# Casting the keys' first bfloat16 part on GpSimd instead of VectorE in a fused gated MLP, attention and MLP block

## The chip, the cores and the metric

The kernel runs on one core of one Trainium2 chip. The metric is the device time of one launch in microseconds (us), the median of several runs. The engines are called as in the profile: PE is TensorE (PEld its weight loads), DVE is VectorE, ACT is ScalarE, POOL is GpSimd and SP is SyncE, which here only starts DMAs.

## The reference

The input is x of shape (32, 128, 128): 32 sequences of 128 tokens of width 128. Two layers follow each other, all in float32:

```
x = x + quantized_down( val * gelu(gate) )          # val, gate = up(x * scale * rsqrt(mean(x*x) + 1e-6))
g1, b1, g2, b2, a1, a2 = condition (six vectors of 128 per sequence)
h = layernorm(x) * g1 + b1
q, k, v = split(h @ W_qkv.T + b_qkv)                # 16 heads of width 8
o = softmax(q @ k.T / sqrt(8)) @ v
x = x + (o @ W_o.T + b_o) * a1
h = layernorm(x) * g2 + b2
x = x + (gelu_tanh(h @ W_f1.T + b_f1) @ W_f2.T + b_f2) * a2
```

## The kernel before

The work is done per sequence b (0 to 31), and in groups g of four sequences (0 to 7) where 512 columns fit one instruction. Three stages follow each other on every engine, and each engine's order is written out by hand as a program of its own, with semaphores between them. An engine carries out its program strictly in order, so an instruction that waits holds up everything behind it on that engine.

The first stage (`gated_mlp(s)`, s from 0 to 38) is the gated MLP with its quantization, one sequence entering per step. It also makes the attention's features for each sequence (POOL normalizes pairs of them into `xn_tile`, L1071, PE transposes them, L580, ACT stores them, L664), and every fourth step POOL computes the next four `rstd0` (L1006), which ACT's `gate` (L695) of the step after it needs. In steps 13, 15, 17, 21 and 23 PE projects the queries, keys or values of groups 0 and 1.

The second stage (`attention(b)`, b from -3 to 32) is attention. It overlaps the end of the first for b from -3 to 3, and from b = 4 it stands alone. Scores are computed twice. One pass (`max_scores`, three sequences ahead) only serves the row maxima (DVE, `mx`, L893). POOL splits the negated maxima into three bfloat16 parts (`split_max`, L1040 to L1046), PE transposes them (`transpose_max`, L434), ACT copies them (`m_T`, L743) and SP sends them by DMA into the stacked queries (L349). The second pass (`exp_scores`) then gives scores less their maxima, ACT takes the exponential (`probs`, L727), PE weighs the values (`weigh`), DVE turns the result (`o_turn`, L900, `rinv`, L903), POOL divides it (`o_norm`, L1094, in `scale_output`) and DVE turns it back (L907). PSUM banks rotate: a pair of banks is filled again only when DVE's maxima or ACT's exponential of its previous fill are done.

float32 queries and keys are multiplied as sums of bfloat16 parts. A group's queries q_f and keys k_f (128x512, float32, written by ACT, L679 and L683) are each split into three parts in `q_part` and `k_part`:

- part 0 is the value rounded to bfloat16: for q by DVE in `cast_q` (L811), for k by DVE in `cast_k` (L818, an addition of a broadcast zero, so with two inputs in SBUF);
- POOL subtracts it (q_rest, L1016; k_rest, L1026), rounds the rest (L1018; L1030) and subtracts again (L1022; L1032).

SP sends the parts into the stacks `q_st` and `k_st` by DMAs (L297 and L301), six rows each, as the parts come ready (`second_q_first_k` waits for `k_cast` before the three DMAs of key part 0; it is entered once per group). There are three stacks, and a group's stacks are first read by `max_scores` some nine us after its parts are made.

In the attention stage this work is spread over the four sequences of a group: with b % 4 = 0 DVE casts q and POOL does L1016 and L1018; with b % 4 = 1 DVE casts k between its two maxima, and POOL does, in this order, `split_max`, `scale_output`, L1022 and L1026; with b % 4 = 2 POOL does `split_max`, `scale_output`, L1030 and L1032; with b % 4 = 3 only the DMAs are left. I call these four positions stage 0, 1, 2 and 3 of a group. Groups 2 to 7 are cast here, at b = 1, 5, 9, 13, 17 and 21. Groups 0 and 1 are cast in the first stage: DVE casts k in steps 16 and 24 at the end of its step, and POOL does L1026 at the end of the same step, behind `ystep` (L1059) and the pair of `xn_tile`.

The third stage is the output projection, the second layer norm and the MLP by groups; it holds none of the changed instructions.

PE's order in one `attention(b)` is: exp scores (b, first half), weigh (b-1, second half), max scores (b+3, first half), a projection if one is due, exp scores (b, second half), weigh (b, first half), max scores (b+3, second half), transpose of the maxima of b+2.

Of the kernel before, what the change touches and what calls it, by code (L numbers as in the profile page):

```python
# [10 lines left out]
ALU = mybir.AluOpType  # L11
# [3 lines left out]
P = 128  # L15
# [7 lines left out]
GRP = 4  # L23
GT = GRP * P
NG = B // GRP
# [7 lines left out]
STACKS = 3  # L33
# [93 lines left out]
SHARED = {f: n for n, f in enumerate(f for f in SHARED_FILLS if f[0] not in ("proj", "res", "norm"))}  # L127
# [10 lines left out]
def build(nc, x, first, early, late, cond, out):  # L138
    x_d = x.rearrange("b t d -> t b d")
    out_d = out.rearrange("b t d -> t b d")  # L140
    with ExitStack() as ctx:
        def sb(name, shape, dt=F32):
            return ctx.enter_context(nc.sbuf_tensor(name, shape, dt))

        def sem(name):
            return ctx.enter_context(nc.semaphore(name))

        def sems(name, n):
            return [sem(f"{name}{k}") for k in range(n)]
# [15 lines left out]
        def wl(name):  # L165
            a, b = LATE_AT[name]
            return w_late[:, a:b]
# [28 lines left out]
        zero_c, eps_c = sb("zero_c", [P, 1]), sb("eps_c", [P, 1])  # L196
# [18 lines left out]
        q_f, k_f = sb("q_f", [D, GT]), sb("k_f", [D, GT])  # L215
        q_rest, k_rest = sb("q_rest", [D, GT]), sb("k_rest", [D, GT])
        q_part, k_part = sb("q_part", [D, 3, GT], BF16), sb("k_part", [D, 3, GT], BF16)
# [22 lines left out]
        def bank(n):  # L240
            return psum[:, n, :]
# [16 lines left out]
        shared_mm, shared_set = sem("shared_mm"), sem("shared_set")  # L258

        q_cast, k_cast, q_step, k_step = sem("q_cast"), sem("k_cast"), sem("q_step"), sem("k_step")  # L260
        q_stacked, k_stacked = sems("q_stacked", STACKS), sems("k_stacked", STACKS)
# [14 lines left out]
        def tile_cols(t, b, n=1):  # L276
            return t[:, b * D:(b + n) * D]
# [4 lines left out]
        def k_done(g):  # L282
            return 16 * 6 * (g // STACKS + 1) + (CONST_DONE if g % STACKS else 0)
# [480 lines left out]
        def _(dve):  # L764
            v = nc.vector
# [16 lines left out]
            def mean_squares(g):  # L782
                v.tensor_scalar(ms[:, g * GRP:(g + 1) * GRP], ssq[:, g * GRP:(g + 1) * GRP], 1.0 / D, 1e-6,
                                ALU.mult, ALU.add).then_inc(ms_set, 1)
# [21 lines left out]
            def cast_q(g):  # L806
                dve.wait_ge(shared_set, SHARED["q", g] + 1)
                if g:
                    dve.wait_ge(q_stacked[(g - 1) % STACKS], q_done(g - 1))
                    dve.wait_ge(q_step, 3 * g)  # L810
                v.tensor_copy(q_part[:, 0, :], q_f[:, :]).then_inc(q_cast, 1)  # L811

            def cast_k(g):
                dve.wait_ge(shared_set, SHARED["k", g] + 1)
                if g:
                    dve.wait_ge(k_stacked[(g - 1) % STACKS], k_done(g - 1))
                    dve.wait_ge(k_step, 3 * g)
                v.tensor_tensor(k_part[:, 0, :], k_f[:, :], zero_c[:, :].to_broadcast([P, GT]), ALU.add).then_inc(k_cast, 1)  # L818

            def gated_mlp(s):  # L820
                if 0 <= s - 2 < B:
                    c, n = s - 2, s % 2
                    dve.wait_ge(a_hintT_mm, c + 1)
                    if c >= 2:
                        dve.wait_ge(a_y_mm, c - 1)
                    v.tensor_scalar(hintT[:, n, :, :].rearrange("p a b -> p (a b)"), bank(5).bitcast(I16)[:, 0:FF], -SHIFT, None,
                                    ALU.add).then_inc(a_hintT, 1)
                if 0 <= s - 4 < B:
                    c = s - 4
                    dve.wait_ge(a_x1, c + 1)  # L830
                    v.bn_stats(stats[:, c % 2, :], tile_cols(x_tok, c)).then_inc(a_stats, 1)
                if s < B:
                    n, m = s % 2, s % 4
                    dve.wait_ge(a_gate, s + 1)
                    dve.wait_ge(a_val_mm, s + 1)
                    if s >= 2:
                        dve.wait_ge(a_hrnd, s - 1)
                    v.scalar_tensor_tensor(hid[:, n, :], bank(3 + n), rstd0[:, s:s + 1], gate[:, n, :], ALU.mult, ALU.mult).then_inc(a_hid, 1)  # L838
                    dve.wait_ge(a_hid, s + 1)
                    v.tensor_reduce(amax[:, m:m + 1], hid[:, n, :], X_AXIS, ALU.max, apply_absolute_value=True).then_inc(a_amax, 1)  # L840
                if s == 0:
                    quantize_down()
                if 0 <= s - 3 < B:
                    c = s - 3
                    xs = tile_cols(x_tok, c)
                    dve.wait_ge(a_y_mm, c + 1)
                    dve.wait_ge(a_ystep, c + 1)
                    v.scalar_tensor_tensor(xs, bank(6)[:, 0:D], ystep[:, c % 8:c % 8 + 1], xs, ALU.mult, ALU.add).then_inc(a_x1, 1)
                if s < B:
                    m = s % 4  # L850
                    dve.wait_ge(a_amax, s + 1)
                    v.tensor_scalar(qstep[:, m:m + 1], amax[:, m:m + 1], 1e-5, 1.0 / 127.0, ALU.max, ALU.mult).then_inc(a_qstep, 1)  # L852
                if 0 <= s - 4 < B:
                    c = s - 4
                    dve.wait_ge(a_stats, c + 1)
                    if c >= 4 and c % 2 == 0:
                        dve.wait_ge(a_xn, c - 2)
                    v.bn_aggr(mv[:, c % 4, :], stats[:, c % 2, :]).then_inc(a_mv, 1)
                if s < B:
                    m = s % 4  # L860
                    dve.wait_ge(a_qstep, s + 1)
                    if s >= 4:
                        dve.wait_ge(a_hrnd, s - 3)
                    v.reciprocal(qscale[:, m:m + 1], qstep[:, m:m + 1]).then_inc(a_qscale, 1)  # L864
                if s == 1:
                    dve.wait_ge(wternT_mm, 1)
                    v.tensor_copy(w_ternT[:, :, :].rearrange("p a b -> p (a b)"), bank(5).bitcast(BF16)[:, 0:FF]).then_inc(wternT_set, 1)
                if s % GRP == 2 and s // GRP + 1 < NG:
                    g = s // GRP + 1
                    dve.wait_ge(sq_set, GRP * g)  # L870
                    mean_squares(g)
                if s == 3:
                    dve.wait_ge(mods_mm, 1)
                    dve.wait_ge(late_loaded, 16)
                    for n in range(6):
                        v.tensor_scalar(mods[:, n, :], bank(MISC_BANK)[:, n * B:(n + 1) * B], wl("b_c")[:, n:n + 1], None, ALU.add).then_inc(mods_set, 1)
                if s == 5:
                    dve.wait_ge(bias_mm, 1)
                    v.tensor_copy(b_qk[:, :], bank(MISC_BANK)[:, 0:2]).then_inc(bias_set, 1)
                    v.tensor_tensor(b_ov[:, :], bank(MISC_BANK)[:, 2:3], wl("b_o"), ALU.add).then_inc(bias_set, 1)  # L880
                if s - 1 in EARLY_PROJ:
                    name, g = EARLY_PROJ[s - 1]
                    if name == "q":
                        cast_q(g)
                    if name == "k":
                        cast_k(g)

            def maxima(c, r):
                pair = PAIRS[OWNER[FILL_AT["max", c, r]]]
# [53 lines left out]
            def attention(b):  # L943
                if 0 <= b - 1 < B:
                    normalize(b - 1)
                if 0 <= b + LEAD < B:
                    maxima(b + LEAD, 0)
                g = (b + 8) // GRP
                if b >= 0 and b % GRP == 0 and g < NG:
                    cast_q(g)  # L950
                if b >= 0 and b % GRP == 1 and g < NG:
                    cast_k(g)
                if b == 27:
                    gate_projection(0)
                if b == 28:
                    add_residual(0, MISC_BANK)
                if 0 <= b + LEAD < B:
                    maxima(b + LEAD, 1)
                if 0 <= b - 1 < B:
                    turn_back(b - 1)  # L960
                if b == 28:
                    statistics(0)
                if b == 29:
                    gate_projection(1)
                if b == 30:
                    modulate(0, MISC_BANK)
                    add_residual(1, MISC_BANK)
                    statistics(1)
# [32 lines left out]
        def _(pool):  # L1001
            p = nc.gpsimd
# [19 lines left out]
                p.tensor_tensor(q_part[:, 2, :], q_rest[:, :], q_part[:, 1, :], ALU.subtract).then_inc(q_step, 1)  # L1022

            def k_rest_first(g):
                pool.wait_ge(k_cast, g + 1)
                p.tensor_tensor(k_rest[:, :], k_f[:, :], k_part[:, 0, :], ALU.subtract).then_inc(k_step, 1)  # L1026

# [137 lines left out]
```

## Time and profile before

| | |
|---|---|
| median of 3 runs | 319.92 us (319.9 to 320.2) |
| the profiled execution | 319.64 us |
| its span, first to last instruction | 317.8 us |
| PE busy | 279.6 us (88%) |
| DVE busy | 246.6 us (78%) |
| ACT busy | 186.3 us (59%) |
| POOL busy | 178.6 us (56%) |
| mean granted clock of PE | 0.983 of full speed |

The profile is one execution. Starts are us from the span's start. A granted clock of 1.00 is 2.4 GHz, 0.50 is 1.2 GHz. Matmul ends are modelled, and neighbouring instructions of one engine may overlap by some hundredths of a us in the listing. In a row of the timeline, the bracket says how long the engine had been idle before the instruction and whose work ended that idle time.

### The profile page before, as it was taken

To read this page: it belongs to the slowest core of one execution; us is meant where nothing else is said; L and a number is where in the kernel's file an instruction comes from. 1 tells how busy PE (TensorE), PEld (TensorE's weight loads), DVE (VectorE), ACT (ScalarE), POOL (GpSimd) and SP (SyncE) were. 2 spreads that over 40 slices of the span, in tenths; PEclk is the share of its full clock that TensorE was granted. 3 is DMA by queue.
4 is the path that set the end of the run, shared out by engine and by line. 5 is a ranking of instruction groups with operands and counts; after the bars stand their busy time and mean duration, and the time that the engine had idled before them with its cause. 6 is when DMAs were issued, how large, how long until landed. Compare 5 with 4: busy or idle time off the path is not lost.

```text
span 317.8 us, 8220 instructions
## 1 busy us (share of the span) xinstructions
PE 279.6 (88%) x2892; PEld 154.6 (49%) x2892; DVE 246.6 (78%) x650; ACT 186.3 (59%) x347; POOL 178.6 (56%) x357
## 2 busy tenths in 40 slices
PE   3989998898989576999999989888877999999993
PEld 2454454454445344555656565655443455555441
DVE  5679997877899976598989898998955676676432
ACT  4557997687768564676677777675545222333330
POOL 8032684985896669377878696953334444322300
PEclk9999999999999997899999999999979999999999
DMA  7940000430340004335354444520000011011112
GB/s 238 327 102 4 0 1 3 120 87 2 92 116 2 0 10 113 86 78 143 93 142 104 119 108 112 149 72 8 6 3 3 0 33 33 1 35 33 33 35 66
DMA packets 26216, 21.57 MB, mean 68 GB/s; under 512 B 4384, under 2 KB 25536, under 8 KB 25920
## 3 DMA queue, kind: packets, MB, share of 16 engines
q1 hardware_dynamic: 25744, 20.37, 24.0%
q10 hardware_dynamic: 432, 0.67, 0.7%
q8 instruction: 24, 0.39, 0.6%
q14 instruction: 16, 0.13, 0.1%
HBM read 4.26 MB, written 2.10 MB: 20 GB/s over the span
## 4 chain that ended last, share of the span: by engine, by line
PE 46%; POOL 20%; DVE 17%; issue 11%; ACT 4%; DMA 1%; POOLq 0%; DVEq 0%; ACTq 0%
PE psum L274 39%; DVE mx L893 5%; POOL q_rest L1016 3%; POOL q_part L1018 3%; POOL q_part L1022 2%; POOL k_rest L1026 2%; DVE hid L838 2%; POOL o_norm L1094 2%; POOL xn_tile L1071 2%; DVE o_turn L900 1%; ACT sq L703 1%; PE psum L623 1%; DVE projT L912 1%; PE psum L460 1%; POOL m_rest L1042 1%
## 5 line engine op out<-in xcount | busy, mean ns | idle before, releaser
L893 DVE TENSOR_REDUCE mx<-psum 128x8 f32<-128x1024 f32 x64 | 75.9, 1193 | 10.5 <-PE psum L274 10.3
L727 ACT ACTIVATE probs<-psum 128x1024 f32<-128x1024 f32 x64 | 65.4, 1023 | 9.5 <-PE psum L274 7.9
L274 PE MATMUL psum<-w_early,h0T 128*128 128x512 f32 x128 | 69.3, 627 | 0.0
L760 ACT ACTIVATE g_act<-psum,w_late 128x512 f32<-128x512 f32 x32 | 22.0, 688 | 46.4 <-PE psum L274 46.4
L274 PE MATMUL psum<-probs,v_pad 128*32 128x128 f32 x1024 | 42.4, 285 | 3.3 <-DVE o_turn L900 2.8
L274 PE MATMUL psum<-h2T,w_late 128*128 128x512 f32 x64 | 31.3, 605 | 0.0
L274 PEld LDWEIGHTS psum<-probs,v_pad 128*32 128x32 f32 x1024 | 25.2, 111 | 11.0 <-ACT probs L727 4.4
L274 PE MATMUL psum<-g_act,w_late 128*128 128x512 f32 x64 | 28.8, 592 | 0.0
L838 DVE SCALAR_TENSOR_TENSOR hid<-psum,rstd,gate 128x512 f32<-128x512 f32 x32 | 23.7, 739 | 6.2 <-PE psum L274 3.7
L695 ACT ACTIVATE gate<-psum,rstd 128x512 f32<-128x512 f32 x32 | 22.0, 688 | 8.9 <-PE psum L274 8.5
L274 PE MATMUL psum<-q_st,k_st 64*128 64x128 bf16 x512 | 26.2, 224 | 0.6 <-DVE mx L893 0.5
L1071 POOL TENSOR_SCALAR xn_tile<-x_tok,mv,rstd 128x128 f32<-128x128 f32 x32 | 25.7, 809 | 1.7
L274 PE MATMUL psum<-k_st,q_st 64*128 64x128 bf16 x512 | 25.5, 220 | 0.6 <-DVE mx L893 0.6
L710 ACT ACTIVATE hrnd<-hid,qscale 128x512 f32<-128x512 f32 x32 | 22.9, 716 | 4.5 <-DVE qscale L864 4.3
L1059 POOL TENSOR_TENSOR ystep<-qstep,w_step 128x1 f32<-128x1 f32 x32 | 6.1, 192 | 31.5 <-DVE qstep L852 31.5
L840 DVE TENSOR_REDUCE amax<-hid 128x1 f32<-128x512 f32 x32 | 22.0, 686 | 1.1
L274 PEld LDWEIGHTS psum<-q_st,k_st 64*128 64x128 bf16 x512 | 15.2, 96 | 15.1 <-issue 11.4
L274 PEld LDWEIGHTS psum<-w_early,h0T 128*128 128x128 f32 x128 | 20.5, 200 | 3.1 <-issue 3.1
L274 PEld LDWEIGHTS psum<-k_st,q_st 64*128 64x128 bf16 x512 | 14.5, 94 | 13.5 <-issue 11.6
L994 DVE TENSOR_SCALAR yT<-psum,w_late,mods 128x128 f32<-128x128 f32 x32 | 10.9, 403 | 12.7 <-PE psum L274 12.7
L1100 POOL TENSOR_TENSOR var_e<-mv,eps_c 128x4 f32<-128x4 f32 x8 | 1.6, 201 | 33.7 <-DVE mv L932 33.7
L1094 POOL TENSOR_TENSOR o_norm<-o_turn,rinv 128x128 f32<-128x128 f32 x32 | 15.7, 491 | 7.9 <-DVE rinv L903 7.8
(125 smaller groups left out, 541.3 us busy)
## 6 DMA issues: line engine op xcount, KB each, us to landing
q_st<-q_part SPq DMA_DIRECT2D x48, 128.0 KB
k_st<-k_part SPq DMA_DIRECT2D x48, 128.0 KB, 2.4
x_tok<-x SPq DMA_DIRECT2D x8, 256.0 KB, 7.2
out<-out_t SPq DMA_DIRECT2D x8, 256.0 KB, 2.3
w_late<-late SPq DMA_DIRECT2D x1, 1159.5 KB, 9.1
w_early<-early ACTq DMA_DIRECT2D x2, 256.0 KB, 5.4
k_st<-k_st SPq DMA_DIRECT2D x4, 128.0 KB, 4.9
q_st<-q_st SPq DMA_DIRECT2D x4, 128.0 KB
```

What stands on the lines that cost most here:

```text
L274: return nc.tensor.matmul(o, w, m, start=start, stop=stop, skip_group_check=shares)
L695: nc.scalar.activation(gate[:, n, :], bank(1 + n), ACT.Gelu, scale=rstd0[:, s:s + 1]).then_inc(a_gate, 1)
L710: nc.scalar.activation(hrnd[:, n, :], hid[:, n, :], ACT.Copy, bias=ROUND_UP, scale=qscale[:, c % 4:c % 4 + 1]).then_inc(a_hrnd, 1)
L727: nc.scalar.activation(probs[:, n % 3, :, :, :].rearrange("p f j q -> p (f j q)"), psum[:, pair[0]:pair[1] + 1, :].rearrange("p a b -> p ( ...
L760: nc.scalar.activation(g_act[:, f, :], bank(2 + f % 2), ACT.Gelu_apprx_tanh, bias=wl("b_f1")[:, f:f + 1]).then_inc(c_gelu[f], 1)
L838: v.scalar_tensor_tensor(hid[:, n, :], bank(3 + n), rstd0[:, s:s + 1], gate[:, n, :], ALU.mult, ALU.mult).then_inc(a_hid, 1)
L840: v.tensor_reduce(amax[:, m:m + 1], hid[:, n, :], X_AXIS, ALU.max, apply_absolute_value=True).then_inc(a_amax, 1)
L893: v.tensor_reduce(mx[:, c % 2, :, r, :], psum[:, pair[0]:pair[1] + 1, :].rearrange("p f (j k) -> p f j k", j=4), X_AXIS, ALU.max, negate=T ...
L994: last = v.tensor_scalar(yT[:, s, :], bank(5)[:, s * P:(s + 1) * P], wl("b_f2"), mods[:, 5, b:b + 1], ALU.add, ALU.mult)
L1016: p.tensor_tensor(q_rest[:, :], q_f[:, :], q_part[:, 0, :], ALU.subtract).then_inc(q_step, 1)
L1071: p.tensor_scalar(xn_tile[:, n + e, :], tile_cols(x_tok, c + e), mv[:, n + e, 0:1], rstd[:, n + e:n + e + 1], ALU.subtract, ALU.mult).then ...
L1094: p.tensor_tensor(o_norm[:, :, :, :], o_turn[:, :, 0:16].rearrange("p g (e d) -> p g e d", e=2), rinv[:, :, :].unsqueeze(3).to_broadcast([ ...
```

## The change

DVE no longer casts k. POOL makes key part 0 itself, with the same addition of a zero, at the start of `k_rest_first`, so directly in front of L1026. The three waits that DVE had in front of the cast (k_f written, the previous group's key stack complete, the previous group's parts all made) are now POOL's. `k_cast` is still what SP waits for. Nothing else moves.

```diff
-            def cast_k(g):
-                dve.wait_ge(shared_set, SHARED["k", g] + 1)
-                if g:
-                    dve.wait_ge(k_stacked[(g - 1) % STACKS], k_done(g - 1))
-                    dve.wait_ge(k_step, 3 * g)
-                v.tensor_tensor(k_part[:, 0, :], k_f[:, :], zero_c[:, :].to_broadcast([P, GT]), ALU.add).then_inc(k_cast, 1)
-
...
                     if name == "q":
                         cast_q(g)
-                    if name == "k":
-                        cast_k(g)
...
                 if b >= 0 and b % GRP == 0 and g < NG:
                     cast_q(g)
-                if b >= 0 and b % GRP == 1 and g < NG:
-                    cast_k(g)
...
             def k_rest_first(g):
+                pool.wait_ge(shared_set, SHARED["k", g] + 1)
+                if g:
+                    pool.wait_ge(k_stacked[(g - 1) % STACKS], k_done(g - 1))
+                    pool.wait_ge(k_step, 3 * g)
+                p.tensor_tensor(k_part[:, 0, :], k_f[:, :], zero_c[:, :].to_broadcast([P, GT]), ALU.add).then_inc(k_cast, 1)
                 pool.wait_ge(k_cast, g + 1)
                 p.tensor_tensor(k_rest[:, :], k_f[:, :], k_part[:, 0, :], ALU.subtract).then_inc(k_step, 1)
```

## Rows read from the trace of the kernel before

**Rows 1.** The page: busy time of PE, and the chain that ended last, by engine.
```profile
PE 279.6 (88%) x2892; PEld 154.6 (49%) x2892; DVE 246.6 (78%) x650; ACT 186.3 (59%) x347; POOL 178.6 (56%) x357
PE 46%; POOL 20%; DVE 17%; issue 11%; ACT 4%; DMA 1%; POOLq 0%; DVEq 0%; ACTq 0%
```
**Rows 2.** The chain of work that ended last: start us, us, what.
```profile
167.46 1.16 POOL q_rest L1016
...
168.70 1.04 POOL q_part L1018
...
175.16 3.54 PE psum L274 x66
...
182.27 1.16 POOL q_rest L1016
```
**Rows 3.** Waits, whole span: engine, line, releaser, us in total, times, longest.
```profile
PE psum L434 <- POOL m_part L1046: 7.0, 14, 1.9
```
**Rows 4.** Timeline, group 5: start us, us, engine, line, operation, idle before.
```profile
170.13 0.40 PE L274 MATMUL psum<-k_st,q_st 64*128 64x128 bf16 x8
...
170.69 0.68 DVE L818 TENSOR_TENSOR k_part<-k_f,zero_c 128x512 bf16<-128x512 f32 x1
170.69 0.94 POOL L1094 TENSOR_TENSOR o_norm<-o_turn,rinv 128x128 f32<-128x128 f32 x1
...
171.29 1.22 DVE L893 TENSOR_REDUCE mx<-psum 128x8 f32<-128x1024 f32 x1
...
172.71 1.15 POOL L1026 TENSOR_TENSOR k_rest<-k_f,k_part 128x512 f32<-128x512 f32 x1
...
173.30 3.01 SPq L301 DMA_DIRECT2D k_st<-k_part  x3
...
173.82 0.19 POOL L1040 CAST m_part<-mx 128x16 bf16<-128x16 f32 x1
...
174.92 0.24 PE L434 MATMUL psum<-eye_b,m_part 128*64 128x128 bf16 x1 [0.33 <-POOL m_part L1046]
```
**Rows 5.** POOL's second key part and o_norm by line: duration ns min/median/max, first and last start.
```profile
L1030 POOL TENSOR_TENSOR k_part<-k_rest,zero_c x8: 1036/1040/1043, 63.1 to 204.8; 128x512 bf16<-128x512 f32 x8
L1094 POOL TENSOR_TENSOR o_norm<-o_turn,rinv x32: 406/408/945, 122.6 to 243.3; 128x128 f32<-128x128 f32 x32
```
**Rows 6.** Timeline of POOL, ACT and PE around the key cast of group 0.
```profile
60.10 1.73 POOL L1071 TENSOR_SCALAR xn_tile<-x_tok,mv,rstd 128x128 f32<-128x128 f32 x2
...
68.21 1.03 POOL L1006 TENSOR_TENSOR rstd<-ms,half 128x4 f32<-128x4 f32 x1
...
69.64 0.69 ACT L695 ACTIVATE gate<-psum,rstd 128x512 f32<-128x512 f32 x1 [0.25 <-PE psum L274]
...
74.45 1.10 PE L274 MATMUL psum<-feat,wq_h 128*128 128x512 f32 x2 [0.93 <-ACT feat L664]
```
**Rows 7.** Timeline of POOL and PE around the key cast of group 1.
```profile
85.94 1.79 POOL L1071 TENSOR_SCALAR xn_tile<-x_tok,mv,rstd 128x128 f32<-128x128 f32 x2
...
92.42 1.58 POOL L1071 TENSOR_SCALAR xn_tile<-x_tok,mv,rstd 128x128 f32<-128x128 f32 x2
...
93.28 0.33 PE L580 MATMUL psum<-w_first,xn_tile 128*128 128x128 f32 x1 [1.04 <-POOL xn_tile L1071]
```
**Rows 8.** Timeline of PE and POOL around the key cast of group 2.
```profile
122.68 0.32 PE L434 MATMUL psum<-eye_b,m_part 128*64 128x128 bf16 x1 [1.94 <-POOL m_part L1046]
...
129.75 0.24 PE L434 MATMUL psum<-eye_b,m_part 128*64 128x128 bf16 x1
...
131.15 0.20 POOL L1040 CAST m_part<-mx 128x16 bf16<-128x16 f32 x1 [2.19 <-DVE mx L893]
```
**Rows 9.** Windows of the span: busy us (x) by engine, granted PE clock, DMA share, GB/s.
```profile
120.00:122.00 2.00, 0.75 (x24) 0.37 (x15) 2.00 (x3) 0.73 (x1) 1.91 (x4) 1.00 0.72 185
...
124.00:126.00 2.00, 2.00 (x33) 1.19 (x29) 0.46 (x2) 1.41 (x2) 1.78 (x5) 0.50 0.34 88
...
170.00:210.00 40.00, 36.75 (x743) 23.26 (x739) 36.27 (x60) 28.13 (x41) 32.47 (x74) 1.00 0.49 127
```

## The prediction

> **What bounds the kernel now.** I first read the page's busy shares and its chain [rows 1]. PE is busy for 88% of the span, but the chain of work that ended last runs through PE for only 46%, through POOL for 20% and DVE for 17%. POOL is busy for only 56% of the span, yet carries a fifth of the chain: it must be late at certain places. Since this change takes 8 instructions from DVE and gives 8 to POOL, those places decide.
>
> So I read the chain in order of time [rows 2]. In the attention stage it repeats: q_rest starts at 167.46 and again at 182.27, one group of four sequences in 14.81 us, and the same steps stand there for five groups (q_rest at 137.84, 152.65, 167.46, 182.27 and 197.09). Within a group the chain enters POOL at q_rest, stays on it up to k_rest, goes to 3.54 us of PE work, then over DVE's maxima and cast of q back to POOL. The waits view has the hand-over: PE waits 7.0 us in all, 14 times, for POOL's last part of the maxima [rows 3]. The timeline shows where in the group [rows 4]: k_rest runs from 172.71, split_max follows without idle time at 173.82, and PE's transpose at 174.92 has stood idle 0.33 us for it. Everything that makes k_rest end later makes that transpose, and all of PE behind it, later by the same amount. DVE is not in that stretch: its second maxima of stage 1 start at 171.29, right behind the cast of k, though PE's scores for them were done at 170.53 [rows 4]. The cast does hold DVE up there, by 0.6 us, but split_max of the next stage starts only at 173.82, long after these maxima end at 172.51. DVE's time there is cover, POOL's is not.
>
> **The change, part by part.**
>
> *DVE without the cast.* Eight times 0.68 us [rows 4], 5.4 us of busy time. In the attention groups I cost the gain at 0: the maxima get ready 0.6 us earlier for a POOL that comes 1.3 us later. In the first stage DVE waits for PE soon after each of the two casts. What this would be worth if DVE were the bound is a rival below.
>
> *o_norm gets its speed back.* o_norm takes 0.94 us at 170.69, where the cast of k starts on DVE at the same moment [rows 4]; its median over 32 is 0.408 us and its maximum 0.945 us [rows 5]. That is 0.53 us on POOL, in the stretch without idle time that ends at PE's transpose, and so on the path. The change removes the DVE instruction that does it: -0.53 us per group. It is the one thing that speaks for the change. The Trainium skill (SBUF — State Buffer, Who interferes with whom) says that a DVE instruction with two SBUF inputs contends with a GpSimd one that reads SBUF, and that the second to issue fully blocks until the first finishes. By that rule the slip would be up to the cast's whole 0.68 us, which would make the forecast some 0.8 us lower over five groups; the measured duration shows 0.53, and that decides.
>
> *POOL with the cast.* The same form (128x512 bfloat16 from float32, adding the zero) takes POOL 1.040 us, 1.036 to 1.043 [rows 5]. k_rest now also waits for POOL's own preceding instruction. Such a pair in the chain, q_rest at 167.46 with 1.16 us and its follower at 168.70, leave a gap of 0.08 us [rows 2]; an instruction that waits for nothing recent starts some 0.03 us ahead of its predecessor's end (173.82 against 172.71 + 1.15 [rows 4]). So the cast costs 1.04 + 0.11 = 1.15 us of POOL. The three added waits are for things long done (k_f, the last group's stack and steps), and I cost them at 0, between 0 and 0.05 us each group; the first part of the maxima at 173.82 has two satisfied waits and follows its predecessor without a gap [rows 4].
>
> *Groups 3 to 7.* 1.15 - 0.53 = +0.62; worked forward from 170.69 with 0.41, 1.16, 1.04, the gap and k_rest, and overlaps as in the rows, k_rest ends 0.58 us later. I take 0.58: PE's idle time of 0.33 us at the transpose [rows 4] becomes about 0.9. It closes a ring, so each group pays it: 5 x 0.58 = +2.9 us. Bounds: 0.3 a group if the ring has some slack that I don't see, 0.7 if every wait costs.
>
> *Group 2.* PE waits 1.94 us at 122.68 for POOL and then runs at half clock; its next transpose at 129.75 does not wait, and POOL itself is idle 2.19 us before 131.15 [rows 8]. POOL's extra 1.15 us fits into that idle time. A little is won since the DVE cast no longer runs beside POOL: -0.1 us.
>
> *Group 1 (step 24).* The pair of xn_tile at 85.94 takes 1.79 us beside the DVE cast, 1.58 without [rows 7]: -0.21. The cast adds 1.04 + 0.08, together +0.91 us, behind it. From there POOL has no idle time up to the next xn_tile, for which PE already stands idle 1.04 us at 93.28 [rows 7]. All of it is on the path: +0.9 us.
>
> *Group 0 (step 16).* The same sum, 1.12 - 0.15 = +0.97 us on POOL (the pair at 60.10 takes 1.73). POOL's next product that someone waits for is rstd0: it ends at 69.24, and ACT's gate starts at 69.64, released by PE [rows 6]. With 0.97 us more it ends at 70.21, and the gate starts some 0.6 us later. ACT runs without idle time from there until the features that PE's projection at 74.45 has waited 0.93 us for [rows 6]. So +0.6 us; 0 to 0.97 as bounds.
>
> *SP's queue.* key part 0 is ready some 1.8 us later than now, at about 173.2. SP gets to its wait for k_cast after the two DMAs of q, and starts the keys' DMAs at 173.30 [rows 4]. The queue's own work hides it: 0. If that cover fails, the maxima's DMA behind it moves by a few tenths, and its reader comes two sequences later.
>
> **Sum:** 2.9 - 0.1 + 0.9 + 0.6 = +4.3 us. The sum is made against the profiled execution, 319.64 us, which is 0.3 us below the median; I add it to the median of 319.92 and get 324.2 us.
>
> **PE's clock** is the large unknown. Before 122.68 PE had stood still for 1.94 us (0.75 us busy of the two from 120 to 122), then its granted clock was 0.50, the lower of its two levels, from 124 to 126 [rows 8, 9]. From transpose to transpose (122.68 to 129.75) that is 7.07 us, where a group has four such stretches in 14.81 us, 3.70 each. The difference is 3.4 us; this stretch has the projection of the values and, in the overlap, one transpose more in it, so I estimate the loss at 2.5 us. The idle time of 1.04 us at 93.28 becomes about 1.95 us, as long as the one that lost the clock. On the other hand the existing loss may become shorter or go away, since everything shifts. Bounds of the net effect: -2.5 to +2.5 us; I take 0.
>
> **Rivals.**
>
> *A second clock loss,* at the stall near 93.3. For it: the idle time would equal the one that lost the clock. Against: the stall of 1.04 us at 93.28 [rows 7] went without loss, and one case doesn't show that length alone decides. Forecast plus 1.3 to 2.5 us: 325.5 to 326.7 us, say 326.0. Chance 0.25.
>
> *The existing clock loss gets shorter or goes,* with the same POOL delays: 324.2 less 1 to 2.5 us, 321.7 to 323.2. Chance 0.15.
>
> *Half the delay is absorbed:* the ring has slack, or the delay of group 0 meets no one. 0.3 x 5 + 0.9 - 0.1 = +2.3 us: 322.2. Chance 0.1.
>
> *Faster:* DVE is the bound of the attention stage, not POOL. Then 0.6 us of earlier maxima per group counts, and POOL's cast would fall into idle time. Where: at PE's transpose of stage 2. The point from which it decides: POOL would have to reach it 1 us before PE, where now it comes 0.33 us after. PE's idle time of 0.33 us would go in five groups: -1.6 us, 318.3 us. For it: DVE is busy for 36.3 of the 40 us from 170 to 210, POOL for 32.5 [rows 9]. Against: each of the five groups shows PE waiting for POOL there and no wait for DVE. Chance 0.05.
>
> *Nothing measurable,* gain and loss cancelling within 0.2%, 319.3 to 320.6 (a measurement of this kernel tells no more than about 0.2%): the speed of o_norm back is worth as much as the cast. That needs the cast to cost under 0.6 us on POOL where the same form takes 1.04. Chance 0.04.
>
> **How the numbers follow.** The POOL case as summed up has 0.41, a second clock loss 0.25, a smaller loss 0.15, half absorbed 0.1, no change 0.04, faster 0.05. The likeliest gives 324.2. The range takes in the clock cases down to 322.0 and up to 326.7, and leaves out about 0.15. Slower by over 0.2%: 0.91; within: 0.04; faster: 0.05.
>
> **What would show it.** Right: in the new profile the cast on POOL takes 1.04 us; o_norm has no duration of 0.94 any more, only 0.41; a group takes 15.4 us instead of 14.81; PE's idle time ahead of the transpose of stage 2 is 0.9 us; DVE shows more idle time and is waited for by no one; PE's idle time near 94 is about 1.9. Wrong: a group still takes 14.8 us, or POOL idles before split_max of stage 2. The clock's windows near 94 and 124 would show which of the clock cases holds.

## The result and the profile after

The changed kernel takes 324.98 us (median of 6 runs, 323.12 to 326.04), against 319.95 us of the kernel before. The ratio is 1.0153, with a 95% interval of 1.0122 to 1.0183: 5.0 us slower, 3.9 to 5.9 by the interval. Forecast were 324.2 us and a range of 322.0 to 326.7. The profiled execution took 325.1 us, with a span of 323.3, 5.5 more than before. Here and below medians are of all runs, while ratios leave out runs more than 1.5% above the fastest of the same kernel, the worst of which took 397.4 us at a mean granted clock of 0.66 (the changed kernel with a copy on POOL).

The page of the kernel after, where one line gives busy time by engine and one the chain that ended last:

```profile
PE 281.0 (87%) x2892; PEld 155.2 (48%) x2892; DVE 243.1 (75%) x642; ACT 186.5 (58%) x347; POOL 183.3 (57%) x365
PE 45%; POOL 24%; DVE 16%; issue 10%; ACT 3%; DMA 1%; POOLq 0%; DVEq 0%; ACTq 0%
```

Against [rows 1] DVE has 3.5 us less to do and POOL 4.7 more, and POOL's share of the chain goes from 20% to 24%: 63.6 to 77.6 us by those shares. POOL's 4.7 are eight casts of 1.04 (8.3), less the 2.65 that the five slow o_norm lose, 0.4 of the two pairs of xn_tile, and about half a us that I did not place. DVE's 3.5 is less than the 5.4 of its eight casts; the rest was not looked into. The lines of the key parts and of o_norm (durations in ns, min/median/max, first and last start) answer to [rows 5]:

```profile
L1018 POOL TENSOR_TENSOR k_part<-k_f,zero_c x8: 1035/1039/1039, 61.8 to 207.2; 128x512 bf16<-128x512 f32 x8
L1088 POOL TENSOR_TENSOR o_norm<-o_turn,rinv x32: 405/407/409, 125.6 to 248.7; 128x128 f32<-128x128 f32 x32
```

The cast costs what the same form cost elsewhere on POOL. o_norm's maximum fell from 0.945 to 0.409 us: not one of the 32 is slow any more. The timeline of POOL, and then of DVE, SP and PE, in group 5 answers to [rows 4]:

```profile
174.93 0.41 POOL L1088 TENSOR_TENSOR o_norm<-o_turn,rinv 128x128 f32<-128x128 f32 x1
175.29 1.16 POOL L1011 TENSOR_TENSOR q_part<-q_rest,q_part 128x512 bf16<-128x512 f32 x1
176.40 1.04 POOL L1018 TENSOR_TENSOR k_part<-k_f,zero_c 128x512 bf16<-128x512 f32 x1
177.52 1.16 POOL L1020 TENSOR_TENSOR k_rest<-k_f,k_part 128x512 f32<-128x512 f32 x1
178.62 0.20 POOL L1034 CAST m_part<-mx 128x16 bf16<-128x16 f32 x1
...
178.86 1.22 DVE L884 TENSOR_REDUCE mx<-psum 128x8 f32<-128x1024 f32 x1 [0.81 <-PE psum L274]
...
177.54 2.53 SPq L301 DMA_DIRECT2D k_st<-k_part  x3
...
179.73 0.24 PE L434 MATMUL psum<-eye_b,m_part 128*64 128x128 bf16 x1 [0.91 <-POOL m_part L1040]
```

POOL goes without a gap from o_norm to the maxima's first part. From o_norm's start to that part's it takes 3.69 us, where it took 3.13 before, and PE's idle time ahead of the transpose is 0.91 us instead of 0.33. DVE now waits 0.81 us for PE before its second maxima of stage 2, where it waited 0.22 before the change:

```profile
174.63 1.23 DVE L893 TENSOR_REDUCE mx<-psum 128x8 f32<-128x1024 f32 x1 [0.22 <-PE psum L274]
```

The time that it was given turns into waiting. SP's queue is busy with the DMAs of q until 177.50 (176.32 + 1.18), the cast ends at 177.44 and the keys' DMAs start at 177.54. So the queue hid the later cast, with 0.06 us to spare. The chain has one group in 15.39 us instead of 14.81:

```profile
156.30 1.16 POOL q_rest L1005
...
171.69 1.16 POOL q_rest L1005
```

The first stage, timeline of POOL, ACT and PE, answers to [rows 6, 7]:

```profile
69.33 1.03 POOL L995 TENSOR_TENSOR rstd<-ms,half 128x4 f32<-128x4 f32 x1
...
70.44 0.69 ACT L695 ACTIVATE gate<-psum,rstd 128x512 f32<-128x512 f32 x1 [0.86 <-POOL rstd L995]
...
75.17 1.10 PE L274 MATMUL psum<-feat,wq_h 128*128 128x512 f32 x2 [1.15 <-ACT feat L664]
```
```profile
94.89 0.46 PE L580 MATMUL psum<-w_first,xn_tile 128*128 128x128 f32 x1 [2.10 <-POOL xn_tile L1065]
...
95.36 1.91 PE L274 MATMUL psum<-w_early,h0T 128*128 128x512 f32 x2
```

ACT's gate, before released by PE, is now released by POOL's rstd0, 0.86 us idle instead of 0.25. PE stands idle 2.10 us before 94.89, and its next two products take 1.91 us, where such a pair took 1.02 before (93.55). The windows show why. Each row has the window, its length, the busy us of PE, PEld, DVE, ACT and POOL, the granted clock, the DMA share and GB/s:

```profile
94.00:96.00 2.00, 1.11 (x3) 0.81 (x4) 1.25 (x6) 0.61 (x2) 1.96 (x4) 0.74 0.38 107
96.00:98.00 2.00, 2.00 (x7) 1.02 (x6) 0.27 (x1) 0.80 (x3) 1.81 (x5) 0.50 0.00 0
98.00:100.00 2.00, 2.00 (x10) 0.84 (x9) 1.23 (x4) 1.22 (x3) 1.52 (x2) 0.91 0.00 0
```

From within 94 to 96 to within 98 to 100 PE ran at 1.2 GHz. So this execution had the rival's second clock loss as well. The second profiled execution of the same kernel, below, has it too, in the same windows.

Where the 5.5 us of span went, read as the shift of the same instruction between the two traces:

| instruction | before | after | shift | of it new |
|---|---|---|---|---|
| first q_rest | 54.37 | 54.53 | 0.16 | 0.16, before any change |
| PE's projection, q of group 1 | 74.45 | 75.17 | 0.72 | 0.56, group 0 |
| L580 waited for by PE | 93.28 | 94.89 | 1.61 | 0.89, group 1 |
| L580, two later | 98.22 | 101.51 | 3.29 | 1.68, half clock after 95 |
| q_rest of group 3 | 137.84 | 140.91 | 3.07 | -0.22, group 2 and the overlap |
| q_rest of group 7 | 197.09 | 202.48 | 5.39 | 2.32, four groups of 0.58 |
| transpose of the maxima, waited for | 208.16 | 214.10 | 5.94 | 0.55, group 7 |
| PE's last transposes | 313.73 | 319.20 | 5.47 | -0.47, end of attention |

The -0.47 comes between two rows of PE, 231.55 (237.50 after) and 239.44 (244.91 after). Both executions have a stretch at half clock there, and what gave the 0.47 back is not shown.

### The profile page after: what moved, and what is told of

The parts are those of the page before. It is cut to its first block, busy times and chain, and to the rows that moved or that the text cites. A ratio compares the mean times of both kernels' runs of the same rounds, so it can differ in the third digit from the quotient of the medians.

```text
span 323.3 us, 8220 instructions
## 1 busy us (share of the span) xinstructions
PE 281.0 (87%) x2892; PEld 155.2 (48%) x2892; DVE 243.1 (75%) x642; ACT 186.5 (58%) x347; POOL 183.3 (57%) x365
## 4 chain that ended last, share of the span: by engine, by line
PE 45%; POOL 24%; DVE 16%; issue 10%; ACT 3%; DMA 1%; POOLq 0%; DVEq 0%; ACTq 0%
PE psum L274 39%; DVE mx L884 6%; POOL q_rest L1005 3%; POOL q_part L1007 3%; POOL k_rest L1020 3%; POOL q_part L1011 2%; POOL k_part L1018 2%; POOL xn_tile L1065 2%; DVE hid L831 2%; PE psum L468 1%; PE psum L623 1%; POOL o_norm L1088 1%; POOL rstd L1062 1%; DVE o_turn L891 1%; PE psum L535 1%
## 5 line engine op out<-in xcount | busy, mean ns | idle before, releaser
L274 PE MATMUL psum<-w_early,h0T 128*128 128x512 f32 x128 | 70.4, 636 | 0.0
L819 DVE TENSOR_SCALAR hintT<-psum 128x512 bf16<-128x512 int16 x32 | 13.5, 422 | 9.7 <-PE psum L535 9.7
```

What stands on the lines that cost most here:

```text
L274: return nc.tensor.matmul(o, w, m, start=start, stop=stop, skip_group_check=shares)
```

## The experiments

**Halves of the change.** The cast of k moves to POOL for some groups only.

```diff
             def cast_k(g):
+                if g < 2:              # the other kernel: g >= 2
+                    return
...
             def k_rest_first(g):
+                if g < 2:              # the other kernel: g >= 2
+                    (POOL's waits and cast of the changed kernel)
```

Early groups alone:

> Only the key casts of groups 0 and 1 (first stage) are on POOL, those of groups 2 to 7 stay on DVE. My theory (POOL is on the path, PE's clock reacts to the longer stall near 94): group 0 costs 0.6 us, group 1 0.9 us, and a PE stall of about 2 us near 94 is followed by half clock for 1.7 us more: 1.5 us without the clock loss, 3.0 with it, so 321.5 to 323.0; groups in the attention stage keep 14.81 us and o_norm its 0.94. Rival (the early casts hide, all of the loss is in the attention stage): 320.0.

322.2 us against 319.6 (ratio 1.0079, 1.0041 to 1.0117), 2.5 us more by the ratio. Late groups alone:

> Only the key casts of groups 2 to 7 (attention stage) are on POOL, groups 0 and 1 stay on DVE. My theory: five groups cost 0.58 us each, group 2 nothing, no clock loss near 94: plus 2.8 us, 322.7, and 15.39 us per group. If the changed kernel's loss were mostly the clock's, plus 1 us or less. e1 and e2 together should give the changed kernel's loss of about 5 us if the two halves are independent.

321.84 us (ratio 1.0072, 1.0037 to 1.0107), 2.3 us more, where 2.8 was expected. The two losses add up to 1.51%, the changed kernel's 1.53%; with intervals of 0.35 to 0.4% each, so close a match is partly chance. In the profile of the second kernel group after group starts 15.39 us after the last, as foretold; in the first it is 14.81, apart from one group of 15.14 (to 184.70) and one of 14.79 behind it. At the end of the long one POOL waits 1.17 us for DVE's cast of q instead of 0.83; what made DVE late is open. So about half of the loss comes from two instructions of the first stage and half from the attention stage. The two are on the path for 0.56 and 0.89 us; the 1.0 us by which 2.5 exceeds their sum is not placed.

In the group that starts at 184.70 the key cast meets another instruction of POOL than o_norm, which is of use below:

```profile
187.60 0.68 DVE L820 TENSOR_TENSOR k_part<-k_f,zero_c 128x512 bf16<-128x512 f32 x1
187.76 0.60 POOL L1054 TENSOR_TENSOR m_part<-m_rest,m_part 128x16 bf16<-128x16 f32 x1
```

The profile of the first kernel (early groups on POOL) shows something that I had not expected. PE's wait there, and the clock in windows near it and later:

```profile
94.66 0.33 PE L580 MATMUL psum<-w_first,xn_tile 128*128 128x128 f32 x1 [2.10 <-POOL xn_tile L1079]
```
```profile
94.00:96.00 2.00, 1.34 (x8) 0.77 (x9) 1.05 (x5) 0.71 (x2) 2.00 (x4) 1.00 0.29 82
96.00:98.00 2.00, 2.00 (x14) 1.05 (x12) 1.30 (x3) 1.39 (x3) 1.81 (x5) 1.00 0.00 0
112.00:114.00 2.00, 1.90 (x11) 0.85 (x10) 2.00 (x5) 0.46 (x1) 1.86 (x4) 0.50 0.04 8
```

The same stall of 2.10 us, to the hundredth, and the clock stays at full speed. PE's shift against the kernel before is 1.38 us at the stall's end (94.66) and 1.39 two L580 later (99.61), where the changed kernel's grew by 1.68: that term is the half clock's. Later the clock is at half between 110 and 120, where the profiled execution of the kernel before had none. The long stall isn't needed for that: the kernel with the late groups on POOL, whose stall near 94 is 1.04 us as before, has it too:

```profile
112.00:114.00 2.00, 1.69 (x10) 0.35 (x9) 1.49 (x2) 0.69 (x1) 0.83 (x5) 0.50 0.01 4
```

The half clock after 95 was seen only behind the stall of 2.10 us, in two of the three profiles with that stall; the length alone does not decide it.

**The form of DVE's cast.** What makes o_norm slow?

```diff
-                v.tensor_tensor(k_part[:, 0, :], k_f[:, :], zero_c[:, :].to_broadcast([P, GT]), ALU.add).then_inc(k_cast, 1)
+                v.tensor_copy(k_part[:, 0, :], k_f[:, :]).then_inc(k_cast, 1)
```

> All casts stay on DVE, but as a copy (as for q, 0.41 us) and not as an addition of zero with two inputs (0.68). Theory A (the slip of o_norm is the length of the DVE instruction that holds what both share): o_norm beside it takes 0.65 to 0.75 us instead of 0.94, PE's wait of 0.33 at the transpose of stage 2 shrinks by 0.2 to 0.3, five times: minus 1.0 to 1.5 us, 318.5 to 319. Theory B (only an instruction with two SBUF inputs collides): o_norm 0.41, minus 1.6 us. Theory C (o_norm's 0.94 has another cause): no change, 319.9.

317.75 us, ratio 0.9938 (0.9906 to 0.9971): 2.0 us less than the kernel before, a little more than any of the theories had. Timeline of DVE and POOL:

```profile
169.07 0.41 DVE L818 CAST k_part<-k_f 128x512 bf16<-128x512 f32 x1
169.08 0.67 POOL L1094 TENSOR_TENSOR o_norm<-o_turn,rinv 128x128 f32<-128x128 f32 x1
```

Theory A holds by the durations. Beside a DVE cast of 0.68 us o_norm is 0.53 longer than its 0.41, beside one of 0.41 it is 0.26 longer: in both cases the slip is DVE's duration less 0.15. The case at 187.60 above fits too: POOL's m_part, 0.22 us elsewhere, started 0.16 us after the cast and is 0.38 longer, with 0.68 - 0.16 - 0.15 = 0.37. That is one instruction standing still until the other is nearly through; were POOL only slowed to a fixed rate, the slip would be the same share of DVE's duration, and it is 0.78 of it in one case and 0.63 in the other. Where POOL comes first it is spared: in the group that starts at 151.28 o_norm started 0.20 us ahead of the cast and kept its 0.41, the cast took 0.49, and POOL's instruction behind it 1.34 instead of 1.16.

The Trainium skill (SBUF — State Buffer, Who interferes with whom) has it that DVE and GpSimd share one pair of ports as an exclusive lock, which a DVE instruction with two SBUF inputs needs against a GpSimd one that reads, and which a copy or cast can take in its two-port modes; the later one fully blocks. The traces agree with the block for both forms: the slips are 0.53 of 0.68 us and 0.26 of 0.41. My forecast had set the whole 0.68 aside for the 0.53 measured, and the 0.15 is what keeps slip and duration apart here. In which mode the copy ran no run shows. A group takes 14.53 to 14.57 us, 0.27 less; only the first of the four is 14.93, with a wait of PE for the maxima's DMA (0.54 us at 148.02).

**The cast on ACT,** so that neither DVE nor POOL has it in the attention stage (DVE's `cast_k` does nothing for groups 2 to 7):

```diff
                 if on:
                     exps(b, 1)
+                g = (b + 8) // GRP
+                if b >= 0 and b % GRP == 1 and g < NG:
+                    (three waits)
+                    nc.scalar.copy(k_part[:, 0, :], k_f[:, :]).then_inc(k_cast, 1)
```

> The key casts of groups 2 to 7 go to ACT, in stage 1 behind its second exponential, where it stands idle 0.69 us; groups 0 and 1 stay on DVE. If POOL's stretch is what PE waits for, and the DVE cast beside o_norm is 0.53 us of it: o_norm 0.41 everywhere, PE's wait at the transpose of stage 2 gone (0.33 us, five times), minus 1.6 us, 318.3; the rest of the 0.53 is slack. If ACT's cast of 0.6 to 0.7 us delays m_T or the exponentials, minus 0 to 1. If DVE were the bound (rival), minus 3 us or more, since DVE loses 0.6 us per group.

317.92 us, ratio 0.9945 (0.9915 to 0.9974), 1.8 us less where 1.6 was expected. ACT's cast and the two instructions of POOL and PE that matter:

```profile
169.95 0.61 ACT L744 CAST k_part<-k_f 128x512 bf16<-128x512 f32 x1
...
170.36 0.41 POOL L1102 TENSOR_TENSOR o_norm<-o_turn,rinv 128x128 f32<-128x128 f32 x1
170.46 0.24 PE L434 MATMUL psum<-eye_b,m_part 128*64 128x128 bf16 x1 [0.26 <-POOL m_part L1054]
```

Two groups take 14.41 us, 0.40 less than before, and PE has no wait for POOL in stage 2 any more. The last takes 14.50 and the first 14.93, in which PE waits for something new, the DMA that brings the maxima into the stack:

```profile
141.81 0.40 PE L274 MATMUL psum<-q_st,k_st 64*128 64x128 bf16 x8 [0.45 <-DMA q_st<-m_T]
```

Now that POOL no longer holds PE up, this transfer is what comes late in one group of the four. DVE is relieved by 0.68 us a group here just as in the changed kernel, and the gain is that of PE's wait, 0.33, and 0.07 more, far from the 3 us in all that DVE as the bound would have given: DVE was not the bound.

**One more cast on POOL,** on top of the kernel before, to see whether POOL's stretch has slack:

```diff
                 pool.wait_ge(k_cast, g + 1)
+                if g >= 2:
+                    p.tensor_tensor(k_part[:, 1, :], k_f[:, :], zero_c[:, :].to_broadcast([P, GT]), ALU.add)
```

> The kernel before (DVE casts k, beside o_norm) with one more cast of the same form on POOL in front of the first key rest, for groups 2 to 7; its output is overwritten, so it is pure cost. The slip of o_norm stays. If the ring has no slack, a group takes 14.81 + 1.12 = 15.93 us, that is 0.54 more than in the changed kernel: the two terms, 1.12 for the cast and 0.53 for the slip, stand apart. If POOL had slack that the changed kernel used up, a group takes less.

One run: 323.13 us; a group takes 15.81 to 15.82 us, not 15.93, with o_norm at 0.94. PE's wait in stage 2:

```profile
160.76 0.24 PE L434 MATMUL psum<-eye_b,m_part 128*64 128x128 bf16 x1 [1.33 <-POOL m_part L1048]
```

The wait grew from 0.33 to 1.33 us: the whole cast went through. It cost 1.00 us and not 1.12: k_rest follows this cast after 1.00 us, start to start (157.55 to 158.55), and it doesn't wait for it, since its output is not read there; in the changed kernel k_rest waits for the cast and follows after 1.12 (176.40 to 177.52). So the change's 0.58 per group is 1.12 less 0.53, within the hundredths of the overlaps, and each term has been seen by itself.

**POOL's cast as a copy,** in the changed kernel, run beside the changed kernel itself:

```diff
-                p.tensor_tensor(k_part[:, 0, :], k_f[:, :], zero_c[:, :].to_broadcast([P, GT]), ALU.add).then_inc(k_cast, 1)
+                p.tensor_copy(k_part[:, 0, :], k_f[:, :]).then_inc(k_cast, 1)
```

> The changed kernel itself, on the same chip as the three below, as their base: 1.5% over the kernel before, 324 to 325.5, groups of 15.39 us.

> The changed kernel, with POOL's cast as a copy (one input) instead of an addition of zero (two inputs). If POOL's time for the addition is set by its two inputs, the copy takes 0.5 to 0.6 us, a group falls from 15.39 to about 14.9 us, and the whole by 2.2 (five groups) plus 0.9 (groups 0 and 1) us: about 1% under the changed kernel, near the kernel before. If POOL's time is set by the 512 elements alone, the copy takes 1.04 and nothing changes.

The changed kernel: 324.91 us, ratio 1.0142 (1.009 to 1.0193), groups of 15.39. With the copy: 320.89 us, ratio 1.0046 (1.0013 to 1.0079), groups of 14.94. Its line:

```profile
L1018 POOL CAST k_part<-k_f x8: 606/609/610, 61.3 to 201.4; 128x512 bf16<-128x512 f32 x8
```

0.609 us instead of 1.039 for the same 512 elements and the same values. So the zero isn't free, though it is one element broadcast; the two forms differ in the kind of instruction as well as in the number of inputs, and the runs don't separate these. The Trainium skill (GPSIMD Engine Reference, Engine selection) puts GpSimd at about twice VectorE's time for work with two inputs, and roughly at line rate for one input. The traces differ: POOL takes 1.5 times as long as DVE in both forms, 1.04 against 0.68 us and 0.61 against 0.41, and the measurement decides. The copy recovers 4.0 of the change's 5.3 us by the medians of this comparison (324.91 less 320.89, of 324.91 less 319.65), two thirds by the ratios.

This run also tells form and place apart. With the key cast as a copy and all else as it was, the kernel has the ratio 0.9938 with the cast on DVE and 1.0046 with it on POOL, and the intervals lie apart; a group takes 14.54 and 14.94 us. So the place costs 0.40 us a group and about 1.1%, 3.4 us, in all even for a copy, where it cost 5.0 us for the addition. The larger part of the change's loss is the place; the form adds to it.

**Work for PE in the stall near 94,** in the changed kernel:

```diff
                     c = s - LN_LAG
+                    if c == 20:
+                        shared_free("ln", c)
+                        for _ in range(32):
+                            mm(bank(MISC_BANK)[:, 3 * P:4 * P], eye_b[:, :], w_ternT[:, 0, :])
                     pe.wait_ge(a_xn, c + 1)
```

> The changed kernel, with 32 products of 128 columns into an unused part of a bank in front of PE's wait for POOL near 94 (1.8 us of the 2.1 us stall; their result is never read). If the half clock after 94 comes from that stall, it is gone: 1.7 us less in executions that had it, in the median 0.5 to 1.7 under the changed kernel. If the clock loss has nothing to do with the stall, the half clock stays and the time is the same or 0.1 more.

323.72 us, ratio 1.0138 (1.0103 to 1.0172), against 324.91 us and 1.0142 of the changed kernel beside it. The medians are 1.2 us apart, the ratios not at all, and the interval of the changed kernel spans 1%: whether it gains is unclear. PE and two windows of the profiled execution, which took 325.53 us, the longest of the twelve:

```profile
92.50 1.95 PE L274 MATMUL psum<-w_ternT,eye_b 128*128 128x128 bf16 x32
94.81 0.33 PE L584 MATMUL psum<-w_first,xn_tile 128*128 128x128 f32 x1 [0.35 <-POOL xn_tile L1069]
```
```profile
96.00:98.00 2.00, 2.00 (x15) 1.15 (x13) 1.15 (x3) 1.25 (x3) 1.81 (x5) 1.00 0.00 0
112.00:114.00 2.00, 1.90 (x11) 0.84 (x10) 2.00 (x5) 0.46 (x1) 1.85 (x4) 0.50 0.04 8
```

The half clock near 96 is gone, but one stands near 112 in this execution. The kernel with only the early groups on POOL also kept the full clock near 96, and without any such work, so this one profile doesn't show that the work did it. The expected gain of 0.5 to 1.7 us is neither shown nor excluded.

**Versions that beat both kernels.** If POOL's stretch and the form of its casts are what counts, all the zero additions should be copies:

```diff
-                p.tensor_tensor(q_part[:, 1, :], q_rest[:, :], zero_c[:, :].to_broadcast([P, GT]), ALU.add).then_inc(q_step, 1)
+                p.tensor_copy(q_part[:, 1, :], q_rest[:, :]).then_inc(q_step, 1)
...
-                p.tensor_tensor(k_part[:, 1, :], k_rest[:, :], zero_c[:, :].to_broadcast([P, GT]), ALU.add).then_inc(k_step, 1)
+                p.tensor_copy(k_part[:, 1, :], k_rest[:, :]).then_inc(k_step, 1)
```

First with all three on POOL, that is the change as it was made but with copies:

> The changed kernel with all three of POOL's casts as copies (keys' first part, rest of q, rest of k). By POOL's stretch: cast 0.43 and q's second part 0.43 less per group, 15.39 - 0.86 = 14.53 us a group, that is 0.28 under the kernel before, five times 1.4; groups 0 and 1 at or under the kernel before: 1.5 to 2.5 us under it, 317.5 to 318.3. So the place of the cast would not be what costs, but its form. Rival (the place costs whatever the form): at or above the kernel before.

316.22 us, ratio 0.9883 (0.9843 to 0.9923), groups of 14.50 as expected: 3.7 us under the kernel before by the ratio. The time is 1.3 us under the range expected, and that part is not placed. The expectation's conclusion, that form and not place is what costs, doesn't follow: two of the three copies replace additions that stay on POOL in every kernel, and would help with the cast on DVE as well, which was not run. The pair compared above shows a cost of the place. Then with the late key casts on ACT, the early ones on DVE as a copy:

> ACT casts the keys of groups 2 to 7 as in the run before with ACT, and the three casts that were additions of zero are copies: on POOL those of q_rest and k_rest (1.04 us each, a copy took 0.61 there), on DVE the early keys. Theory (POOL's stretch in stages 0 and 1 sets PE's waits): PE's remaining waits of 0.26 us for the maxima in stage 1 go, a group falls from 14.41 to about 14.15 us, and PE's wait near 93 loses 0.9: minus 2 us against the run with ACT, 3.5 to 4 us under the kernel before, 315.5 to 316. Rival (PE and DVE are the bound by now): the same as the run with ACT, minus 1.8 us.

314.77 us, ratio 0.9838 (0.9813 to 0.9863), groups of 14.37. Of the groups I had expected 14.15: PE's waits of 0.26 us for POOL's m_part in stage 1 did go, but the group gained only 0.04 on 14.41, for right behind the transpose of that stage PE now waits for DVE's maxima:

```profile
168.42 0.40 PE L274 MATMUL psum<-q_st,k_st 64*128 64x128 bf16 x8 [0.22 <-DVE mx L901]
```

Here the rival was right for the attention stage; the gain came elsewhere. The second q_rest comes at 79.80 instead of 80.22, the third at 115.36 instead of 116.61, and PE waits 0.52 us near 92 instead of 1.04 near 93, a gain of 0.5 where 0.9 was expected. What bounds a group at 14.37 beyond this wait is not settled. Last, the same with work for PE ahead of four of its waits:

```diff
-                pe.wait_ge(b_m, 4 * c + 4)
                 shared_free("m", c)
+                for _ in range({0: 10, 1: 8, 3: 24, 31: 20}.get(c, 0)):
+                    mm(bank(MISC_BANK)[:, 3 * P:4 * P], eye_b[:, :], w_ternT[:, 0, :])
+                pe.wait_ge(b_m, 4 * c + 4)
```

> As the first of this call, with products whose results are never read ahead of four of PE's waits for the maxima (10, 8, 24 and 20 of 128 columns, up to 1.35 us each) in the overlap of first and second stage and near 230. If PE's idle time there costs it the clock, the stretch of 7 to 10 us at half clock between 108 and 130 goes or shrinks, 1 to 2.5 us less than the first of this call. If other idle time of that stretch (104 to 120) decides, no change or 0.5 us more.

314.15 us, ratio 0.9826 (0.9797 to 0.9855). The window from 120 to 130, first of the run without this work, then with it:

```profile
120.00:130.00 10.00, 8.22 (x103) 5.55 (x105) 4.41 (x7) 4.44 (x8) 6.53 (x15) 0.66 0.34 91
```
```profile
120.00:130.00 10.00, 9.12 (x163) 6.05 (x159) 6.30 (x10) 5.99 (x11) 7.30 (x18) 1.00 0.50 129
```

In the profile with the work the clock stays full through the overlap, and q_rest of group 3 comes 2.65 us earlier (133.56 against 136.21). More runs than the profiled one show it: the mean granted clock of its six runs is 0.991 to 1.000, of the five without the work 0.975 to 0.988. In the medians 0.6 us is left, where 1 to 2.5 was expected, and it lies inside the intervals. The four pieces of work are not free: of the 2.65 us 0.5 go in one longer group (PE waits 0.43 us for the maxima's DMA in it), and 0.9 more between the last q_rest and the end.

## Why the prediction was right

- *What bounds the kernel* was read rightly. POOL's stretch up to the transpose of stage 2 had no slack: one more cast went through whole (1.33 - 0.33 = 1.00 us), and taking 0.53 us out gave 0.40: PE's wait of 0.33 us and 0.07 more.
- *DVE without the cast* is worth nothing in the attention stage: the maxima of DVE wait for PE instead (0.81 us in stage 2). In the first stage there is a small gain, where PE's shift fell from 0.72 to 0.55 us between 75 and 92; this is also why the stall near 94 was 2.10 and not 1.95 us. The prediction had DVE waiting for PE soon after each of the two early casts. For the second that was misread; in the kernel before, DVE's next wait for PE is this one:

```profile
86.36 0.69 DVE L818 TENSOR_TENSOR k_part<-k_f,zero_c 128x512 bf16<-128x512 f32 x1
...
94.84 0.42 DVE L826 TENSOR_SCALAR hintT<-psum 128x512 bf16<-128x512 int16 x1 [0.45 <-PE psum L535]
```

The kernel with DVE's cast as a copy agrees: its PE is 0.20 us ahead of the kernel before at 74.25 and 0.36 ahead when it reaches the wait near 92.

- *o_norm gets its speed back*: -0.53, as put.
- *Groups 3 to 7*: forecast 0.58 us each, measured 14.81 to 15.39.
- *Group 2* was put at -0.1. The overlap in which it lies gave -0.22 in all, of which no part is singled out.
- *Groups 1 and 0*: forecast 0.9 and 0.6, measured 0.89 and 0.56, the second by the mechanism named (rstd0 late for ACT's gate).
- *SP's queue*: hidden, as put.
- *The clock* was the term that was mis-sized. I took its net as 0, and in both profiled executions of the changed kernel the half clock after 95 is there. In the one above it cost 1.68 us. The likeliest case, the waits of POOL with no net effect of the clock, had a chance of 0.41; what the profiles show is those waits together with the second clock loss, the rival that I gave 0.25. That rival's times were 325.5 to 326.7 us, and the range was wide enough to take it in.
- *The sum.* Without the clock it was 4.3 us forecast; by the table without the half clock, the -0.47 behind attention and the start it is 0.56 + 0.89 - 0.22 + 2.32 + 0.55 = 4.1 us. The measured 5.0 is 0.7 above the forecast. It lies between the sum without the clock and the profile's 5.5, and the interval of 3.9 to 5.9 takes in the one and the other, so the runs don't fix what the clock adds on average. The waits were right by their mechanism; that the single figure came within 0.8 us although the clock's term was wrong is partly luck. The runs spread from 323.12 to 326.04 us, while the group time is the same to 0.01 us in both profiles; that the clock makes this spread is not shown.

## What to carry to other kernels

An engine at 56% can be the bound: ask which instruction the wait of the fullest engine ends on, and whether the engine it belongs to had any gap back to its own last wait. Before moving a cast, write it as a copy: the addition of a broadcast zero is slower on either engine, on POOL 1.04 against 0.61 us, on DVE 0.68 against 0.41, and on DVE it held up POOL's o_norm for 0.53 us against 0.26. Then compare places with the form held fixed: as a copy the key cast still cost about 1.1% more on POOL than on DVE. An engine that is relieved beside the path, as DVE in the attention stage, gains idle time.

## What was not expected of the hardware

- A copy on POOL of 128x512 float32 to bfloat16 takes 0.609 us, the addition of a broadcast zero 1.039 us.
- The slip of POOL's o_norm is the length of DVE's cast less 0.15 us, for the form with two inputs (0.68: 0.53) and for the copy (0.41: 0.26). It shows as a longer duration of POOL's instruction, not as idle time before it.
- The same stall of PE, 2.10 us at the same place of the program, lost the clock in two of three profiled executions and kept it in one. The two that lost it are of one kernel, and the one that kept it of another, so this doesn't tell chance from the program.
- The places of half clock in the overlap differ from kernel to kernel (110 to 120, or 122 to 133), and are the same in the two profiles of the changed kernel. The runs of the kernel before lay between 316.6 and 322.2 us in the comparisons of the experiments, with mean granted clocks of 0.962 to 0.992, where the first three had lain within 0.3 us. That the clock makes this spread is not shown, since only one of its executions has a profile here. A narrow first set of runs was no proof of a narrow kernel.
